# V's transpose moved from TensorE to VectorE and a DRAM scratch, and float32 logits in place of the split in three products

## What is computed

```
xn = groupnorm(x, 32 groups)                               # 128 images, 384 x 196
q, k, v = conv1x1_bn(xn)                                   # 256, 256 and 1024 channels: 8 heads, 32, 32, 128
vl = depthwise_conv3x3(v) * s + t                          # 1024 channels
attn = q k^T * 32**-0.5 + bias                             # per head 196 x 196
attn = mix_heads(attn, th1) ; softmax ; mix_heads(., th2)  # 8 x 8 talking heads
o = relu(attn v + vl)
y = x + conv1x1_bn(o)                                      # 384 channels
```

## Time and profile before

| | us |
|---|---|
| median of 3 runs | 4813.72 (4812.78 to 4814.12) |
| the profiled execution | 4811.84 |
| its span, first to last instruction | 4810.0 |
| PE busy | 4779.1 (99%) |
| PE weight loads busy | 4760.2 (99%) |
| DVE busy | 4175.9 (87%) |
| ACT busy | 3251.4 (68%) |
| POOL busy | 988.6 (21%) |

### The profile page before, as it was taken

The page is one execution under the profiler, slowest core; times in us unless marked ns, Lnnn a source line. Parts: engine busy times, 40 slices in busy tenths (PEclk is TensorE's granted clock), DMA queues, the critical chain, the costliest instruction groups (busy, mean ns, idle before and its releaser), DMA issues.

```text
span 4810.0 us, 111468 instructions
## 1 busy us (share of the span) xinstructions
PE 4779.1 (99%) x35842; PEld 4760.2 (99%) x35842; DVE 4175.9 (87%) x10897; ACT 3251.4 (68%) x8005; POOL 988.6 (21%) x1093
## 2 busy tenths in 40 slices
PE   7999999999999999999999999999999999999999
PEld 7999999999999999999999999999999999999999
DVE  8888888889888898888888988889888888898887
ACT  6666666666667666667666666766666766666665
POOL 3212212121121221221212212122121221221211
PEclk9999999999999999999999999999999999999999
DMA  1000000000000000000000000000000000000000
GB/s 57 26 20 30 19 26 30 15 30 25 20 30 15 30 25 20 30 15 30 30 15 30 25 20 30 15 30 25 20 30 15 30 29 16 30 21 24 30 15 26
DMA packets 55148, 120.23 MB, mean 25 GB/s; under 512 B 3650, under 2 KB 5842, under 8 KB 55124
## 3 DMA queue, kind: packets, MB, share of 16 engines
q1 hardware_dynamic: 55124, 119.93, 7.4%
HBM read 81.38 MB, written 38.54 MB: 25 GB/s over the span
## 4 chain that ended last, share of the span: by engine, by line
PE 98%; DVE 1%; issue 0%; DMA 0%; ACT 0%; SPq 0%; DVEq 0%
PE psA L250 43%; PE psA L399 14%; PE psL L250 12%; PE psM L250 10%; PE psM L377 8%; PE psL L377 6%; PE psM L367 2%; PE psL L367 2%; DVE psC L620 1%; PE psA L268 0%; PE psA L263 0%; DMA qa<-in_wqkv 0%; DVE probs L675 0%; DVE x_lo L601 0%; DVE q_lo L650 0%
## 5 line engine op out<-in xcount | busy, mean ns | idle before, releaser
L620 DVE SCALAR_TENSOR_TENSOR psC<-vpad,par,psC 128x406 f32<-128x406 f32 x3072 | 1808.7, 637 | 0.0
L498 ACT ACTIVATE probs<-probs,nmax 112x196 f32<-112x196 f32 x1792 | 799.0, 449 | 649.0 <-DVE nmax L675 641.8
L250 PE MATMUL psA<-x_hi,w_lo 128*128 128x392 f32 x2304 | 795.0, 345 | 8.5 <-DVE x_lo L601 8.5
L250 PE MATMUL psA<-x_lo,w_hi 128*128 128x392 f32 x2304 | 788.9, 342 | 0.0
L250 PE MATMUL psA<-x_hi,w_hi 128*128 128x392 f32 x2304 | 788.1, 342 | 0.0
L399 PE MATMUL psA<-qa,shared 105*128 105x196 f32 x4096 | 693.9, 330 | 3.0 <-DVE shared L719 3.0
L399 PEld LDWEIGHTS psA<-qa,shared 105*128 105x128 f32 x4096 | 680.2, 191 | 3.3 <-DVE shared L719 3.3
L650 DVE SCALAR_TENSOR_TENSOR q_lo<-q,th,q_hi 128x392 fp32r<-128x392 f32 x1024 | 604.4, 621 | 34.6 <-ACT q_hi L442 27.6
L719 DVE TENSOR_TENSOR shared<-psA,shared 128x392 f32<-128x392 f32 x512 | 290.1, 567 | 366.5 <-PE psA L399 366.5
L442 ACT ACTIVATE q_hi<-q,th 128x392 fp32r<-128x392 f32 x1024 | 582.0, 620 | 6.0
L434 ACT ACTIVATE o_hi<-shared 128x392 fp32r<-128x392 f32 x512 | 271.5, 530 | 457.6 <-DVE shared L719 457.6
(11 more groups left out here) (85 smaller groups left out, 10500.0 us busy)
## 6 DMA issues: line engine op xcount, KB each, us to landing
xs<-in_x SPq DMA_DIRECT2D x64, 588.0 KB, 3.8
shared<-in_x SPq DMA_DIRECT2D x64, 588.0 KB, 3.8
out<-shared SPq DMA_DIRECT2D x63, 588.0 KB, 3.0
qa<-in_wqkv SPq DMA_DIRECT2D x3, 768.0 KB, 6.7
stage_wp<-in_wp SPq DMA_DIRECT2D x1, 1536.0 KB, 9.9
out<-shared SPq DMA_DIRECT2D x3, 196.0 KB, 2.0
shared<-in_abx SPq DMA_DIRECT2D x1, 165.4 KB
par<-in_par SPq DMA_DIRECT2D x1, 70.5 KB
```

Source lines behind the costliest of these rows:

```text
L250: last = nc.tensor.matmul(dst, w, r, start=(begin and n == 0), stop=(end and n == 2))
L498: nc.scalar.activation(row, row, ACT.Exp, bias=nmax[:, img, b:b + 1], scale=-1.0, accum_out=rowsum[:, img, b:b + 1]).then_inc(s_exp, 1)
L620: nc.vector.scalar_tensor_tensor(a if tap == 7 else sums, src, taps[:, c, TAPS[tap]:TAPS[tap] + 1], a if tap == 0 else sums, MUL, ADD).the ...
```

## The change

Logits: `q_hi`, `q_lo`, `k_hi` and `k_lo` go. ScalarE writes the mixed queries once, in float32 (`mixed_q`, 16 instructions as before), and a bank of logits is 4 float32 matmuls (`mixed_q` stationary, `k` moving) in place of 12 float32r ones. VectorE's 16 L650 products, ScalarE's 2 copies and GpSimd's 2 subtractions go.

V: the 8 "vt" uses and their ScalarE copies go. VectorE transposes each image's V in 32x32 blocks with one instruction (`turn`, 128 partitions by 8 channel tiles by 7 blocks of 32, 1792 elements a partition), written with a step of 8 elements (32 bytes). SP writes it to a DRAM tensor in 4 transfers an image and reads it back in 2, into `vt`. There the channels of a head lie 8 elements apart, so the stationary operand of attention by V is read with a step of 32 bytes. `turned` shares its place with `x_lo`, `q` and `k`, so GpSimd's `x_low` waits for the first image's transfers. `x_high` moves from the 17th of 22 uses to the 7th of 14.

```diff
@@ VectorE
-                mixed_low(8)
-                convs(6)
-                for _ in range(8):
-                    mixed_low(1)
-                    convs(1)
-                convs(1)
+                convs(15)
...
+                def turn(img):
+                    at_ = PITCH + 1 + img * PITCH * PITCH
+                    nc.vector.transpose(turned[:, img, :, :, :].rearrange("p b n c -> p c b n"),
+                                        vpad[:, :, at_:at_ + BLOCKS * BLK].rearrange("p c (b k) -> p c b k", b=BLOCKS)
+                                        ).then_inc(s_turned, 1)
...
-                convs(3)
+                turn(0)
                 dve.wait_ge(s_exp, 28 * t + 28)
                 nc.vector.reciprocal(rinv[:, 1, :], rowsum[:, 1, :]).then_inc(s_rinv, 1)
-                convs(3)
+                turn(1)
                 if not first:
                     project_out(t, 2)
                 convs(64)
@@ TensorE
-                            mm = split3(logit_bank(n)[:, (b - b0) * PIX:(b - b0 + 1) * PIX],
-                                        q_lo[:, img * RES + b, kt, :], q_hi[:, img * RES + b, kt, :],
-                                        k_lo[:, kt, px], k_hi[:, kt, px], kt == 0, kt == QT - 1)
+                            mm = nc.tensor.matmul(logit_bank(n)[:, (b - b0) * PIX:(b - b0 + 1) * PIX],
+                                                  mixed_q[:, img * RES + b, kt, :], k[:, kt, px],
+                                                  start=(kt == 0), stop=(kt == QT - 1))
...
-                for use in range(22):
+                for use in range(14):
...
-                    pe.wait_ge(s_vt_sb, 8 * t + 4 * img + 4)
+                    pe.wait_ge(s_vt_in[img], 32 * (t + 1))
...
-                                                      vt[0:HALF, img, jc, g * D:(g + 1) * D], attn[:, img, jc, g, :],
+                                                      vt[0:HALF, img, jc, :, g], attn[:, img, jc, g, :],
@@ SyncE
+            def turned_out(t, img):
+                sp.wait_ge(s_turned, 2 * t + img + 1)
+                rows = by_key[img].rearrange("(b r) a n -> r a b n", r=BLK)
+                for a in range(P // BLK):
+                    sp.dma_start(rows[:, a, :, :],
+                                 turned[a * BLK:(a + 1) * BLK, img, :, :, :].rearrange("p b n c -> p b (n c)")
+                                 ).then_inc(s_vt_out[img], 16)
+
+            def keys_in(t, img):
+                sp.wait_ge(s_vt_out[img], 16 * (P // BLK) * (t + 1))
+                for jc in range(2):
+                    sp.dma_start(vt[0:ROWS, img, jc, :, :].rearrange("p n c -> p (n c)"),
+                                 by_key[img, jc * HALF:jc * HALF + ROWS, :, :].rearrange("k a n -> k (a n)")
+                                 ).then_inc(s_vt_in[img], 16)
...
+                turned_out(t, 0)
+                turned_out(t, 1)
+                keys_in(t, 0)
+                keys_in(t, 1)
                 if not first:
                     store(t)
@@ GpSimd
-                for kt in range(QT):
-                    wait_alone(pool, s_khi, 2 * t + kt + 1)
-                    nc.gpsimd.tensor_tensor(k_lo[:, kt, :], k[:, kt, :], k_hi[:, kt, :].bitcast(f32),
-                                            SUB).then_inc(s_klo, 1)
...
-                    pool.wait_ge(s_v_mm, VT * (t + 1))
+                    wait_alone(pool, s_vt_out[0], 16 * (P // BLK) * (t + 1))
```

More of the change, by code:

```diff
@@ L19 @@
 HALF = RES // 2 * PITCH
+ROWS = 112
+BLK = 32
+BLOCKS = 7
+PART = VT * BLK
 HR = P // KD
@@ L29 @@
 EPS = 1e-5
+Q_AT = 2 * CT * PIX
+K_HI_AT = Q_AT + QT * COLS
+K_AT = K_HI_AT + QT * COLS
 GAP = 2 * RES * QT * HP - VT // 2 * ACC - 4 * DH
@@ L76, in build @@
         x_hi = sb("x_hi", [P, 2, CT, PIX], f32r)
[L77 to L83, removed]
+        x_lo = over("x_lo", [P, 2, CT, PIX])
+        front = sb("front", [P, 2 * BLOCKS * PART])
         qa = sb("qa", [P, 4 * RES * HP])
@@ new lines, in step @@
+                    else:
+                        pe.wait_ge(s_mix_sb, 14 * t + use - 3)
+                    pe.wait_ge(s_exp, 28 * t + 14 * img + 2 * n + 2)
+                    pe.wait_ge(s_mixw, 8 * t + 4 * img + group(2 * n + 1) + 1)
+                    bank = mix_bank(use)[:, 0:4 * HP].rearrange("p (j g b i) -> p j g b i", j=2, g=NH, b=2)
+                    for jc in range(2):
+                        for b in range(2):
+                            mm = nc.tensor.matmul(bank[:, jc, :, b, :],
+                                                  probs[0:HP + 1, img, 2 * n + b, jc * HALF:(jc + 1) * HALF],
+                                                  mixw[0:HP + 1, img, 2 * n + b, :].rearrange("p (g i) -> p g i", g=NH),
+                                                  start=True, stop=True)
@@ L457, in step @@
                     if m == 0 and not first:
-                        act.wait_ge(s_qlo, 16 * t)
-                    if m == 2 and not first:
                         act.wait_ge(s_logit_mm, 14 * t)
@@ L502, in step @@
                         conv_centre(t, CENTRES[n])
-                for use in range(22):
-                    img, (what, n) = use // 11, USES[use % 11]
-                    if what == "vt":
-                        jc, cg = divmod(n, 2)
-                        act.wait_ge(s_vt_mm, 8 * t + 4 * img + n + 1)
-                        if use == 0 and not first:
-                            act.wait_ge(s_av_mm, 8 * t)
-                        nc.scalar.copy(vt[0:HALF, img, jc, cg * BANK:(cg + 1) * BANK],
-                                       mix_bank(use)).then_inc(s_vt_sb, 1)
-                    else:
-                        act.wait_ge(s_mix_mm, 14 * t + 7 * img + n + 1)
-                        src = mix_bank(use)[:, 0:4 * HP].rearrange("p (j g m) -> p j g m", j=2, g=NH)
-                        nc.scalar.copy(attn[:, img, :, :, 2 * n * RES:(2 * n + 2) * RES], src).then_inc(s_mix_sb, 1)
-                    if use == 16 and not last:
+                for use in range(14):
+                    img, n = divmod(use, 7)
+                    act.wait_ge(s_mix_mm, 14 * t + use + 1)
+                    if use == 0 and not first:
+                        act.wait_ge(s_av_mm, 8 * t)
+                    src = mix_bank(use)[:, 0:4 * HP].rearrange("p (j g m) -> p j g m", j=2, g=NH)
+                    nc.scalar.copy(attn[:, img, :, :, 2 * n * RES:(2 * n + 2) * RES], src).then_inc(s_mix_sb, 1)
+                    if use == 6 and not last:
                         act.wait_ge(s_v_mm, VT * (t + 1))
@@ L639, in step @@
                     stats(t + 1)
-                if not first:
-                    dve.wait_ge(s_olo, 8 * t)
-                    dve.wait_ge(s_av_mm, 8 * t)
-                low_half = iter([(kt, g) for kt in range(QT) for g in range(NH)])
-                def mixed_low(count):
-                    for _ in range(count):
-                        kt, g = next(low_half)
-                        dve.wait_ge(s_qhi, 16 * t + 8 * kt + g + 1)
-                        dst, src = mixed(kt, g)
-                        nc.vector.scalar_tensor_tensor(q_lo[dst], src, th1[:, kt, g:g + 1], q_hi[dst].bitcast(f32),
-                                                       MUL, SUB).then_inc(s_qlo, 1)
+                def turn(img):
[3 more added lines that the diff above has]
+                                        ).then_inc(s_turned, 1)
                 if first:
```

56 lines of the change are left out of this document (24 added, 32 removed).

## The result

The changed kernel takes 5404.0 us (median of 4, 5401.0 to 5406.7). The kernel before, on the same chip, takes 4813.9 (4812.8 to 4814.2). The ratio is 1.1226, with an interval of 1.1207 to 1.1246: slower by 590 us, or 590 / 63 = 9.4 us in each pair but the first. That is outside the main case (5190 to 5330) and inside the range (5050 to 5440). Both things that the prediction named as signs of being wrong came: PE hardly waits for the additions (2.1 us, once in the run), and it waits for V's transfers first.

What follows compares the result with a forecast made beforehand. PE, busy 99%, bounds the kernel. A pair: -3.5 (transposes) + 1.9 (logits) + 6.1 (wait for DVE) + 2.8 (clock) = +7.3 us; 63 pairs give +460, so 5270 us, range 5050 to 5440.

Steps and rivals of the forecast that it cites:

- main case: PE waits for DVE's late additions and its clock drops: +7.3 us a pair, 5270 us, own range 5190 to 5330, chance 0.46.
- the wait that was to give it: PE waits 6.1 us a pair for DVE's first addition, between steps 1 and 2 of attention by V.
- PE's own list: PE's instructions: transposes gone -3.5 us, float32 logits +1.9, so 1.6 us shorter a pair.
- What hides: V's way through DRAM, done some 15 us after the logits and not needed before 21, costs PE nothing.
- E: The moment PE ends a pair's logits; E + 15 means 15 us later.
- Transposes at 2.0: One transpose of V on DVE takes 2.0 us; DVE then reaches the additions 4.1 us too late for PE.
- rival 3: The 32-byte step costs: doubled transposes (4.0 us) give 5390, or weight loads a third slower give 5420; chance 0.15.
- The lock: DVE's two-operand convolution step 49 waits until GpSimd's x_low ends; the additions begin at E + 23.1.
- The clock: PE's granted clock is low behind its gap in attention by V: 2.8 us a pair, bounds 0 and 2.9.
- Rival 1: DVE's step 49 is not held by GpSimd; DVE late by 4.1 us only, +5.2 a pair, 5140; chance 0.15.
- Rival 4: GpSimd holds DVE's transposes for 3 us each: 4.0 us more a pair, 5520; chance 0.07.
- Rivals 2 and 5: 2: PE's clock stays up, 5100 or 4970, chance 0.09. 5: DVE's transposes 0.8 us or less, 4775 at 0.5, chance 0.05.

Runs made afterwards that it cites:

- logits alone: The kernel before with only the logits' half of the change, V still transposed on PE: 4937.5 us, ratio 1.0258.
- the last kernel: The kernel with pairs of heads, with DVE's project_out(2) moved behind the first 6 convolution steps after the logits: 4737.2 us, ratio 0.9841.
- the early kernel with `x_high` at the seventh copy: The changed kernel with both DVE transposes ahead of the logits, x_high left at the seventh copy: 5441.5 us, ratio 1.1305.
- the early kernels: Two versions of the changed kernel with both transposes ahead of the logits, x_high at the seventh or tenth copy: 5441.5 and 5254.7 us.
- the kernel with pairs of heads: The second early kernel with V laid out in pairs of heads, 8-byte steps and four times as many DRAM rows of 256 bytes: 4967.1 us, ratio 1.032.
- the second early kernel: The changed kernel with both DVE transposes ahead of the logits and x_high moved to the tenth copy: 5254.7 us, ratio 1.0918.

## Right or wrong, by the prediction's steps

- **The number, held in part by luck.** 5404 lies in the range, but 134 us over the 5270 forecast, and the wait that was to give it did not occur. Another wait stood almost where that one would have ended.
- **PE's own list, right.** Logits +1.94 a pair against 1.9 (logits alone). The list of -1.6 showed in the end: the last kernel gains 76.6 / 64 = 1.2. In the middle of its run the logits take 0.15 and attention by V 0.2 more than I had, which is the rest.
- **What hides, wrong, and this step decided which wait PE sees.** I put V's arrival at some E + 15 within E + 10.3 to E + 23, and said that PE would not need it before E + 21. It came at E + 20.2, and PE waited 4.6 us a pair for it. Both figures failed. The arrival: I had 3.5 + 5 + 5. The first transpose ended at E + 5.3, the writes took 6.1, the issues of the second image's writes 0.8 more, and the reads 7.9. I had priced the transfers by rows of single ones, with the engines free, and here they are full. The need: E + 21 rests on 16 instructions at 0.164 us. At the low clock, with the step, they take 16 x 0.322 = 5.2, so PE had to start by about E + 19.1 to reach step 2 with the first addition done, at E + 24.3.
- **The two waits overlap.** By the same estimate PE reaches step 2 at 2431.16 + 5.2, E + 25.3, so V's lateness costs only about 1.0 us beyond what the additions would have cost; the trace books all 4.6 on V. Two kernels agree. With the gap filled, PE waits for the first addition at step 2; with both transposes early, the wait for V is gone and 1.5 to 3.9 us a pair of waits for the additions stand in its place.
- **Transposes at 2.0, wrong for this layout.** 3.57 us with the step of 32 bytes, 2.01 without, 2.03 with 8 bytes. That is rival 3's first half, 4.0 a little too dear. DVE's additions came at E + 23.8. (The prediction's E + 21.1 for transposes of 2.0 is 21.0 by its own terms, which changes nothing.)
- **The lock, right as a mechanism, not in this kernel.** The longer transposes moved step 49 to E + 15.0, behind `x_lo`. It stood exactly where predicted once the transposes took 2.01 us (mean 899 against 642 ns), and again in the early kernel with `x_high` at the seventh copy.
- **The clock, right in kind, too dear in size.** 0.50 for 5.8 us behind the gap, and 1.00 with the gap filled. In the pairs shown its price is 2.7 us, as I took it (2.8), when the loads have no step, and 1.5 in the changed kernel.
- **Weight loads, rival 3's second half, true.** I had a third more, 0.05 an instruction behind the gap; it is 0.239 - 0.164 = 0.075 for all 64, or 4.8 us a pair. Taking the step out of this operand alone gave 220 us, 3.4 a pair, since the low clock then costs more. The note of the Trainium skill that the prediction cites there, on steps over 16 bytes, speaks for both halves of the rival and not against them, and both came true.
- **Rival 1 (5140)**, the lock missing, came true by itself without giving its time. **Rival 4**, GpSimd holding the transposes: not seen. They take 3.4 to 3.7 us beside its work, 3.7 in the early kernels where GpSimd is idle, and 2.0 beside its work without the step. **Rivals 2 and 5** did not occur.

The sum as measured, a pair: -3.5 + 1.94 + 4.8 (loads) + 4.6 (wait for V's reads) + 1.5 (clock) = +9.3, where (5404.0 - 4813.9) / 63 is 9.4. I forecast 7.3. The wait of 6.1 for DVE is not in this sum, since the wait for V's reads, which I had priced at nothing, covers it. The weight loads I had given to rival 3.

Open: how much of V's way is the DMA engines and how much SP's issues was not separated by an experiment. Not tried either: the first image's reads issued ahead of the second's writes, another queue for the second image, and a stepped write of 16 bytes.

## What to carry to other kernels

Before calling a way through DRAM hidden, add up its transfers as they land when others run beside them, not alone, and look which issues stand ahead of the one that is waited for. When two things are late for one engine, ask what the second would cost if the first came in time. Lay out small float32 operands so that the step stays at 8 bytes; here pairs instead of eights gave it at no cost. When a piece of work is taken out of an engine's order, look at what it was covering there: six convolution steps moved into that hole turned 1.032 into 0.984.

## What the runs showed of the hardware

- A stepped stationary float32 operand: load of 128 columns 190 ns (no step), 196 (8 bytes), 329 (16), 336 (32); an instruction of 196 columns 0.166 us (no step) or 0.239 (32 bytes).
- A VectorE 32x32 transpose of 1792 float32 a partition: 2.01 us without a step on the write, 2.03 with 8 bytes, 3.57 with 32. The Trainium skill, "Vector Engine (DVE) Microarchitecture Reference", section 3.8, has one element per cycle, an estimate of 1.9 us; the traces agree for the first two (2.01 and 2.03) and not for the last.
- Two SBUF operands on DVE beside a GpSimd subtraction: two steps 3.28 us instead of 1.2, until it ended. The transpose, with its one SBUF input, was not held (2.04 and 1.98 us beside GpSimd's multiplications).
- A weight load with a step of 32 bytes does not get faster with the clock: 338 ns at 0.50 and 336 at 1.00, where one without a step has 337 and 190.
- Transfers beside others: with the DMA engines at a share of 0.97 to 1.01 a read of 448 KB landed 6.6 us after its issue (median), where 588 KB alone took 3.8.
- An issue by SP takes 0.66 us for such a write and 0.43 for such a read (medians of the changed kernel), 0.47 and 0.40 with the transposes early.
- TensorE's granted clock was 0.50 for part of attention by V in all 62 pairs of the loop behind the gap of some 4.6 us of the changed kernel, in 33 of 62 behind the 2.65 us gap of the kernel with pairs of heads, and in 52 of 62 behind the 1.4 us gap of the second early kernel. So the length of the gap alone does not decide it; what does was not tried.
